# Preparing the feed-forward weights in eighths, inside the turns of the first attention layer

## The chip, the cores and the metric

The kernel runs on one core of a Trainium2 chip. The metric is the device time of one execution in microseconds (us), as the median of several runs. The engines are TensorE (PE; its weight loads are listed as PEld), VectorE (DVE), ScalarE (ACT), GpSimd (POOL) and SyncE (SP), which only issues transfers. A transfer is issued from the queue of an engine (SPq, ACTq, POOLq) and carried by the core's 16 DMA engines. TensorE's granted clock is given as a share of full speed: 1.00 is 2.4 GHz and 0.50 is 1.2 GHz.

## The reference

Two layers over x of 8 batches x 512 positions x 256 features, float32. What matters here is the first:

```
xn = layernorm(x)
x  = x + attention0(xn) + ffn0(xn)          # then a second layer: x + attention1 + mixture of experts

attention0: c = xn @ W_DKV (64 wide); k, v from c; q = xn @ W_UQ
            16 heads of 16, causal, softmax, @ W_O
ffn0:       tlin(x, w, s) = einsum('bsi,oi->bso', x, w) * s
            h = silu(tlin(x, w1)) * tlin(x, w2)         # 256 -> 1024, twice
            h = gelu(tlin(h, h1)); h = gelu(tlin(h, h2)) # 1024 -> 1024
            return tlin(h, w3)                          # 1024 -> 256
```

The weights w1, w2, h1, h2 and w3 hold only -1, 0 and 1 in the inputs used, but the kernel doesn't assume it: it tests at run time whether rounding them loses anything.

## The kernel before

Matrix products keep float32 accuracy by splitting each operand into a rounded part (type fp32r, "high") and what is left ("low"), and adding the products of the parts.

**Layer 0's attention (`latent_attention`)** is a software pipeline over batches. A turn is one batch: 32 steps (`STEPS`), and in each step one score tile (`score`: PE L521 and L526 into PSUM, then the row maximum on DVE, L429) and one probability tile of 13 steps earlier (`prob`: PE L545, exponential on ACT L372, causal cut on POOL L323, and later the value product PE L557). Everything else of a batch is hung on fixed steps by hand, in the table `placed`: loading and normalising the next x (steps 0 to 11), its transpose (`x_turn`, `x_copy`, `x_high`, `x_low`, step 12), v (15), the latent (16), the output's transpose (`mix_turn` and what follows, 17), q and k (`qk`, 18 and 21, with DVE casts L422 `qk_high` and POOL subtractions L313 `qk_low`, 19 and 22), the output product (`out`, 24: PE L483 with l_wo) and its store (`store`, 25, issued by ACT L389). Each engine walks the same list in the same order, and waits only on semaphores, so an instruction put into a step delays all that stands behind it on its engine. Three PSUM slots of two banks go round among `score`, `prob`, `x_turn`, `v`, `qk`, `heads_turn`, `mix_turn` and `out`: a product may start when the reader of the slot three uses back is done (`claim`). So score 21 waits for DVE's maximum of score 20, `out` for that of score 22, and a score whose slot held a probability tile waits for ACT's exponential. The turns are written out for -1, 0, 7 and 8 and looped for 1 to 6.

**Between attention and feed-forward** `clear` resets the semaphores of the attention. Then `ffn` runs three blocks, with all engines meeting between them. The first loads the five weight matrices in 28 chunks of up to 128x1024 into a ring of four (SP L1157), rounds each (ACT L1173), and compares it with its rounding in both directions (DVE L1186, `tensor_tensor_reduce`, which subtracts and keeps the maximum). A transpose on PE (L1207) and two reductions give `flag`, whether anything was lost. The weights' high parts stay in SBUF. Meanwhile `BiasTable` makes a position table for layer 1: POOL loads `wpos`, `coeffs` and `fir` (`t_fir`, 101 rows of 4 KB, L1088), PE multiplies (L1095, L1098), ACT copies (L1103, L1106). The second block writes the low parts to DRAM, if `flag` says so; here it does not. The third loops over the 8 batches: gates and ups (PE L1376, 64 products), h1 and h2 (L1401 with the high part of h, L1411 with the low), w3 (L1446).

Of the kernel before, what the change touches and what calls it, by code (L numbers as in the profile page):

```python
# [15 lines left out]
F32 = mybir.dt.float32  # L16
# [6 lines left out]
P = 128  # L23
B, T, D = 8, 512, 256
KD = D // P
# [70 lines left out]
def latent_attention(nc, x_d, out_d, xh_d, xl_d, w, c):  # L96
# [4 lines left out]
    with ExitStack() as ctx:  # L101
# [40 lines left out]

        slots = [ctx.enter_context(nc.psum_tensor(f"l0_slot{j}", [P, 2, T], F32)) for j in range(3)]
# [24 lines left out]
        out_saved = sem("out_saved", 1, grant=1, unit=16)  # L168
        held_sp, held_dve, held_pool = sem("held_sp"), sem("held_dve"), sem("held_pool")
# [91 lines left out]
        with nc.Block() as block:  # L261
            @block.sync
            def _(sp):
# [34 lines left out]
                sp.dma_start(stacks[HROWS - 1:P:HROWS, 1].bitcast(F32), minus).then_inc(keyed.sem, 16)  # L298
                turns(sp, emit)
# [31 lines left out]
            def _(act):  # L331
# [18 lines left out]
                def emit(kind, b, n, i):  # L350
# [36 lines left out]
                    if kind == "store":  # L387
                        wait(act, out_ready, 1, b)
                        act.dma_start(out_d[b].rearrange("(t p) d -> p t d", p=P), out_sb[:]).then_inc(out_saved.sem, 16)  # L389
                turns(act, emit)  # L390
                act.wait_ge(out_saved.sem, out_saved.at(1, B - 1))

            @block.vector
            def _(dve):
                def emit(kind, b, n, i):
                    if kind == "ln_stats":
# [67 lines left out]
                dve.tensor_tensor(wo[:, 1], raw_wo[:], wo[:, 0].bitcast(F32), ALU.subtract).then_inc(w_ready.sem, 1)  # L464
                turns(dve, emit)

# [122 lines left out]
        clear(nc, tallies)  # L589
# [468 lines left out]

def attention(nc, tag, layer, x_d, out_d, xh_d, xl_d, xn_d, w, c):
    if layer == 0:  # L1060
        latent_attention(nc, x_d, out_d, xh_d, xl_d, w, c)
# [5 lines left out]
class BiasTable:  # L1067
# [5 lines left out]
    def __init__(self, nc, ctx, wpos, coeffs, ext_d, c, banks):  # L1073
        def sb(name, shape):
            return ctx.enter_context(nc.sbuf_tensor(f"t_{name}", shape, F32))

        def sem(name):
            return ctx.enter_context(nc.semaphore(f"t_{name}"))
# [4 lines left out]
        self.loaded, self.cw_ps, self.cw_ready, self.ext_ps, self.ext_ready, self.saved = \  # L1083
            (sem(n) for n in ("loaded", "cw_ps", "cw_ready", "ext_ps", "ext_ready", "saved"))

    def move(self, eng):
        for dst, src in zip((self.wpos, self.coeffs, self.fir), self.sources):
            eng.dma_start(dst[:], src).then_inc(self.loaded, 16)  # L1088
        eng.wait_ge(self.ext_ready, 2)
        eng.dma_start(self.ext_d, self.ext[:].rearrange("h a t -> h (a t)")).then_inc(self.saved, 16)  # L1090
        eng.wait_ge(self.saved, 16)
# [17 lines left out]
def ffn(nc, x_d, attn_d, xh_d, xl_d, out_d, w, c, lo_d, bias):  # L1109
# [5 lines left out]
    with ExitStack() as ctx:  # L1115
        def sb(name, shape, dt=F32):
            return ctx.enter_context(nc.sbuf_tensor(f"f_{name}", shape, dt))

# [6 lines left out]
        names = ("w1", "w2", "h1", "h2", "w3")  # L1125
        wide = {"w1": HID, "w2": HID, "h1": HID, "h2": HID, "w3": D}
        deep = {"w1": KD, "w2": KD, "h1": KH, "h2": KH, "w3": KH}
        hi = {m: sb(f"hi_{m}", [P, deep[m], wide[m]], F32R) for m in names}
        gate_s, both_s, h1_s, h2_s = (sb(n, [P, KH]) for n in ("gate_s", "both_s", "h1_s", "h2_s"))
        out_s = sb("out_s", [P, D])  # L1130
        ident = sb("ident", [P, P])
        flag = sb("flag", [1, 1], mybir.dt.int32)
        low = sb("low", [P, 2, KH, P], F32R)
        psum = [ctx.enter_context(nc.psum_tensor(f"f_ps{j}", [P, T], F32)) for j in range(8)]


        CH, RING = 1024, 4
        chunks = [(m, k) for m in names for k in range(deep[m])]

        loaded = [sem(f"loaded{j}", unit=16) for j in range(RING)]  # L1140
        hi_done, compared = sem("hi_done"), sem("compared")
        raw_in = [sem(f"raw_in{j}", unit=16) for j in range(2)]
        saved = [sem(f"saved{j}", unit=16) for j in range(2)]
        lo_done = sem("lo_done")
        s_in, s_done, peak_ps, peak_done = sem("s_in", unit=16), sem("s_done"), sem("peak_ps"), sem("peak_done")
        with nc.sbuf_tensor("f_raw", [P, RING, CH], F32) as raw, nc.sbuf_tensor("f_junk", [P, 2, CH], F32) as junk, \
             nc.sbuf_tensor("f_peaks", [P, 2, len(chunks)], F32) as peaks, \
             nc.sbuf_tensor("f_peak", [P, 1], F32) as peak, nc.sbuf_tensor("f_any", [1, 1], F32) as top, \
             ExitStack() as inner, nc.Block() as block:
            table = BiasTable(nc, inner, *bias, c, psum[1:4])  # L1150

            @block.sync
            def _(sp):
# [6 lines left out]
            @block.gpsimd  # L1160
            def _(pool):
                pool.dma_start(ident[:], c["c_ident"]).then_inc(s_in.sem, 16)
                for dst, src in ((gate_s, "w1_s"), (both_s, "w2_s"), (h1_s, "h1_s"), (h2_s, "h2_s")):
                    pool.dma_start(dst[:], w[src]).then_inc(s_in.sem, 16)
                s3 = w["w3_s"]
                pool.dma_start(out_s[:], bass.AP(s3.tensor, s3.offset, [[0, P], [1, D]])).then_inc(s_in.sem, 16)
                table.move(pool)

            @block.scalar
            def _(act):  # L1170
                for n, (m, k) in enumerate(chunks):
                    act.wait_ge(loaded[n % RING].sem, 16 * (n // RING + 1))
                    act.activation(hi[m][:, k], raw[:, n % RING, 0:wide[m]], ACT.Copy).then_inc(hi_done.sem, 1)  # L1173
                    if n == len(chunks) // 2:
                        table.copies(act)

            @block.vector
            def _(dve):
                for n, (m, k) in enumerate(chunks):
                    dve.wait_ge(hi_done.sem, n + 1)  # L1180
                    if n:
                        dve.wait_ge(compared.sem, n)

                    pair = raw[:, n % RING, 0:wide[m]], hi[m][:, k].bitcast(F32)
# [822 lines left out]
```

## Time and profile before

| | |
|---|---|
| median of 3 runs | 2241.44 us (2241.33 to 2242.36) |
| the profiled execution | 2235.95 us |
| its span, first to last instruction | 2234.3 us |
| mean granted clock of TensorE | 0.895 |
| busy shares of the span | PE 79%, DVE 50%, ACT 46%, POOL 45% |

The span is from the first instruction to the last; the execution's own time is 1.65 us more, and the median of the plain runs lies 5.5 us above the profiled execution. Times in the rows further down count from the span's start, so attention 0 fills roughly 0 to 504 us, the preparation of the weights 511 to 576, and the feed-forward loop begins at 584.

### The profile page before, as it was taken

The page shows a single profiled execution, that of the slowest core. Times are in us where ns is not written, and L with a number is a line of the kernel's source. Part 1 is how long each engine was busy: PE and PEld are TensorE (multiplying, and loading weights), DVE is VectorE, ACT ScalarE, POOL GpSimd, SP SyncE. Part 2 cuts the span into 40 slices and gives each one's busy share as a digit, 9 for nine tenths or more (in the row PEclk, how much of TensorE's full clock was granted, in tenths as well). Part 3 has the DMA queues.
Part 4 walks back from the last instruction along what each step waited for, and adds up shares of the span by engine and source line. Part 5 has one row for each costly group of instructions (what it writes and reads, how often), then busy time and mean ns, then how long its engine had stood idle before and what let it go on. Part 6 is the DMA issues. An engine that isn't in the chain of part 4 may idle for free. (4 is left out here: it accounts for less than half of the span.)

```text
span 2234.3 us, 33907 instructions
## 1 busy us (share of the span) xinstructions
PE 1764.3 (79%) x10759; PEld 1101.2 (49%) x10759; DVE 1122.0 (50%) x2399; ACT 1024.8 (46%) x1356; POOL 1012.5 (45%) x778
## 2 busy tenths in 40 slices
PE   3888889870599999999999638887887888747933
PEld 2455555540387787787787523333433433235510
DVE  3666666537513313313313148878787787437211
ACT  1455555543313322222223117877787788813400
POOL 3344444320234344343333407777777677724212
PEclk8899999985799999999999858989998999869965
DMA  3333333306201101101100253222222222043999
GB/s 102 87 96 94 94 104 91 94 11 202 84 1 47 47 0 47 47 0 47 45 2 28 77 174 86 67 71 80 80 66 71 81 65 59 10 173 137 345 318 330
DMA packets 129732, 204.38 MB, mean 91 GB/s; under 512 B 14303, under 2 KB 84063, under 8 KB 129668
## 3 DMA queue, kind: packets, MB, share of 16 engines
q1 hardware_dynamic: 107896, 163.40, 24.6%
q10 hardware_dynamic: 16096, 20.65, 2.6%
q0 software_dynamic: 5680, 19.57, 2.2%
q8 instruction: 32, 0.52, 0.1%
q14 instruction: 28, 0.23, 0.0%
HBM read 95.96 MB, written 56.69 MB: 68 GB/s over the span
## 5 line engine op out<-in xcount | busy, mean ns | idle before, releaser
L761 POOL TENSOR_TENSOR l_prob<-l_prob,l_bias 128x1024 f32<-128x1024 f32 x192 | 452.1, 2375 | 149.2 <-ACT l_prob L865 148.4
L1315 POOL TENSOR_TENSOR f_hl<-f_full,f_hh 128x512 fp32r<-128x512 f32 x192 | 247.6, 1290 | 439.9 <-DVE f_hh L1357 283.2
L922 DVE CUSTOM_DVE_ANT_0 l_slot<-l_slot,l_bias 128x512 f32<-128x512 f32 x512 | 340.4, 714 | 52.8 <-PE l_slot L999 51.7
L1357 DVE CAST f_hh<-f_full 128x512 fp32r<-128x512 f32 x128 | 74.8, 585 | 397.7 <-ACT f_full L1336 396.2
L868 ACT ACTIVATE l_prob<-l_prob 128x1024 f32<-128x1024 f32 x256 | 271.1, 1071 | 0.0
L1401 PE MATMUL f_ps<-f_hh,f_hi_h 128*128 128x512 f32 x1024 | 267.1, 397 | 0.0
L1411 PE MATMUL f_ps<-f_hl,f_hi_h 128*128 128x512 f32 x1024 | 265.8, 396 | 0.0
L429 DVE TENSOR_REDUCE l_peak<-l_slot 128x2 f32<-128x256 f32 (+3 forms) x256 | 206.2, 821 | 111.3 <-PE l_slot L526 109.0
L1336 ACT ACTIVATE f_full<-f_ps,f_h_s 128x512 f32<-128x512 f32 x128 | 86.3, 687 | 332.6 <-PE f_ps L1411 308.9
L372 ACT ACTIVATE l_prob<-l_slot 128x1024 f32<-128x1024 f32 (+3 forms) x256 | 174.7, 706 | 96.3 <-PE l_slot L545 93.4
L1401 PEld LDWEIGHTS f_ps<-f_hh,f_hi_h 128*128 128x128 f32 x1024 | 192.8, 188 | 49.3 <-ACT f_hh L1329 2.7
L1411 PEld LDWEIGHTS f_ps<-f_hl,f_hi_h 128*128 128x128 f32 x1024 | 192.9, 188 | 46.6
L865 ACT COPY l_prob<-l_slot 128x1024 f32<-128x1024 f32 x192 | 194.8, 1015 | 34.3 <-PE l_slot L1015 33.6
L323 POOL TENSOR_SCALAR_AFFINE_SELECT l_prob<-l_prob 128x256 f32<-128x256 f32 x256 | 105.0, 418 | 210.1 <-ACT l_prob L372 207.3
L1027 PE MATMUL l_o_bank<-l_prob,l_vals 128*32 128x512 f32 x1024 | 158.3, 694 | 4.7 <-ACT l_prob L868 4.7
L999 PE MATMUL l_slot<-l_stacks 63*128 63x512 f32 x512 | 121.1, 472 | 49.2 <-DVE l_prob L761 23.6
L1015 PE MATMUL l_slot<-l_stacks 64*128 64x512 f32 x512 | 134.5, 524 | 20.9 <-DVE l_peak L922 16.8
L521 PE MATMUL l_slot<-l_stacks 63*128 63x256 f32 (+2 forms) x512 | 98.1, 380 | 32.5 <-ACT l_prob L372 18.1
L1015 PEld LDWEIGHTS l_slot<-l_stacks 64*128 64x128 f32 x512 | 51.5, 199 | 138.3 <-DVE l_peak L922 96.3
L545 PE MATMUL l_slot<-l_stacks 64*128 64x256 f32 (+2 forms) x512 | 109.7, 428 | 10.5 <-DVE l_peak L429 4.1
L557 PE MATMUL l_o_bank<-l_prob,l_vals 128*32 128x512 f32 (+3 forms) x1024 | 97.2, 452 | 11.1 <-POOL l_prob L323 9.7
L1325 ACT ACTIVATE f_tanh<-f_ps,f_gate_s 128x512 f32<-128x512 f32 x64 | 44.1, 688 | 119.5 <-PE f_ps L1376 119.5
(209 smaller groups left out, 2691.5 us busy)
## 6 DMA issues: line engine op xcount, KB each, us to landing
l_stacks<-l_parts SPq DMA_DIRECT2D x384, 128.0 KB, 2.7
inter<-e_stage POOLq DMA_DIRECT2D x32, 512.0 KB, 5.1
c_rows<-inter SPq DMA_DIRECT2D x32, 512.0 KB, 9.6
attn<-l_out_sb ACTq DMA_DIRECT2D x16, 512.0 KB, 2.8
f_raw<-in_L_ffn_h_w SPq DMA_DIRECT2D x16, 512.0 KB, 4.2
e_w<-in_L_ffn_f SPq DMA_DIRECT2D x32, 256.0 KB, 4.4
l_bias<-ext ACTq DMA_DIRECT2D x16, 448.0 KB, 11.8
l_x_in<-in_L_attn_x SPq DMA_DIRECT2D x8, 512.0 KB, 3.8
```

The source lines that it names most:

```text
L372: act.activation(prob[:, n // 2 % RING, 2 * pr:2 * pr + 2, j * P:T], slot(kind, n)[:, :, j * P - q0:wide], ACT.Exp).then_inc(p_exp.sem, 1)
L429: dve.tensor_reduce(peak[:, g, :, pr, t], slot(kind, n)[:, :, 0:(t + 1) * P], AX_X, ALU.max)\
L761: return eng.tensor_tensor(probs(n), src, bias[:, h:h + 2, j * P:j * P + T], ALU.add)
L865: act.copy(probs(n), slot(kind, n)[:]).then_inc(p_copied.sem, 1)
L868: act.activation(probs(n), probs(n), ACT.Exp).then_inc(p_exp.sem, 1)
L922: ins = dve.tensor_tensor_reduce(src, src, bias[:, 4 * g + 2 * pr + a, t * P:t * P + T], 1.0, 3 * NEG, ALU.add, ALU.max, peak[:, g, a, pr, ...
L999: ins = pe.matmul(out[:, a], stacks[r, 0, 2 * g + pr, t * P:(t + 1) * P], stacks[r, 1, 2 * g + pr, ::-1], start=True, stop=True)
L1015: ins = pe.matmul(out[:, a], stacks[r, 1, 2 * g + pr, j * P:(j + 1) * P], stacks[r, 0, 2 * g + pr, ::-1], start=True, stop=True)
L1027: ins = pe.matmul(o_bank[32 * a:32 * a + 32, :], vals_sb[:, v0:v0 + 32], prob[:, n % RING, a], start=(j == 0), stop=(j == TT - 1), skip_gr ...
L1315: pool.tensor_tensor(hl[layer % 2][:, o], full[:, n % 2], hh[layer % 2][:, o].bitcast(F32), ALU.subtract).then_inc(h_lo.sem, 1)
L1401: ins = pe.matmul(hidden[n % 4][:], hi[m][:, k, cut], hh[layer % 2][:, k], start=(k == 0), stop=False, skip_group_check=True)
L1411: ins = pe.matmul(hidden[n % 4][:], hi[m][:, k, cut], hl[layer % 2][:, k], start=False, stop=(k == KH - 1), skip_group_check=True)
```

## The change

The preparation block and the block for the low parts go. Each turn of layer 0's attention now prepares an eighth of every weight matrix (`Prepare`; a row block of 128 of w3, h1 and h2, and a column block of 128 of w1 and w2: 2816 columns in all): ACT issues five loads in step 7, rounds four cuts of 704 columns in steps 12, 13, 15 and 16, and stores the high part in step 18 and the low part in step 26; DVE makes the low part and one maximum in steps 14, 16, 19 and 21, and the maximum of the opposite difference in steps 15, 18, 20 and 22. Both parts are always written, to DRAM. After the last turn the flag is made.

The feed-forward stage is now one block. SP loads x and then the high parts of all weights from DRAM, and PE waits for each where it first needs it. The position table moves into this block: its three loads from POOL's queue to ACT's, its products on PE ahead of the first gate product. The semaphores of the attention are cleared by POOL within the same block, so one meeting of the engines is left between the two stages.

```diff
+        for s, kind, n in ((7, "f_load", 0), (12, "f_round", 0), (13, "f_round", 1), (15, "f_round", 2), (16, "f_round", 3),
+                           (14, "f_low", 0), (15, "f_high", 0), (16, "f_low", 1), (18, "f_high", 1),
+                           (19, "f_low", 2), (20, "f_high", 2), (21, "f_low", 3), (22, "f_high", 3),
+                           (18, "f_save_high", 0), (26, "f_save_low", 0), (27, "f_worst", 0)):
+            placed[s].append((kind, 0, n))
         for s, events in {0: [("x_load", 1, 0)],
...
+                    if kind == "f_load":
+                        wait(act, f_compared, 2 * prep.SPLIT, b - 1)
+                        for m in prep.NAMES:
+                            dst = f_raw[:, prep.columns(m)]
+                            if m in ("w1", "w2"):
+                                dst = dst.rearrange("p (k n) -> p k n", k=KD)
+                            act.dma_start(dst, prep.source(m, b)).then_inc(f_loaded.sem, 16)
+                    if kind == "f_round":
+                        if n == 0:
+                            wait(act, f_loaded, len(prep.NAMES), b)
+                            wait(act, f_saved, 2, b - 1)
+                        cut = slice(n * cut_by, (n + 1) * cut_by)
+                        act.copy(f_high[:, cut], f_raw[:, cut]).then_inc(f_rounded.sem, 1)
+                    if kind == "f_save_high":
+                        wait(act, f_rounded, prep.SPLIT, b)
+                        act.dma_start(prep.high_d[b], f_high[:].bitcast(F32)).then_inc(f_saved.sem, 16)
+                    if kind == "f_save_low":
+                        wait(act, f_compared, 2 * prep.SPLIT, b)
+                        act.dma_start(prep.low_d[b], f_low[:]).then_inc(f_saved.sem, 16)
...
+                            hold(dve, held_dve, f_rounded, n + 1, b)
+                            dve.tensor_tensor_reduce(f_low[:, cut], pair[0], pair[1], 1.0, 0.0, ALU.subtract, ALU.max,
+                                                     peaks[:, 0, n:n + 1]).then_inc(f_compared.sem, 1)
+                        else:
+                            hold(dve, held_dve, f_compared, 2 * n, b)
+                            dve.tensor_tensor_reduce(junk[:], pair[1], pair[0], 1.0, 0.0, ALU.subtract, ALU.max,
+                                                     peaks[:, 1, n:n + 1]).then_inc(f_compared.sem, 1)
...
-        clear(nc, tallies)
+    return tallies
...
-            table = BiasTable(nc, inner, *bias, c, psum[1:4])
-                for n, (m, k) in enumerate(chunks):
-                    if n >= RING:
-                        sp.wait_ge(compared.sem, n - RING + 1)
-                    sp.dma_start(raw[:, n % RING, 0:wide[m]], w[m + "_w"][k * P:(k + 1) * P])\
-                      .then_inc(loaded[n % RING].sem, 16)
...
-                table.move(pool)
...
-                    act.activation(hi[m][:, k], raw[:, n % RING, 0:wide[m]], ACT.Copy).then_inc(hi_done.sem, 1)
...
+        before = latent_attention(nc, *FIRST.pop(), prep)
...
+                sp.dma_start(gates_flat[:, 0], prep.high_d[0, :, both]).then_inc(first_in.sem, 16)
+                sp.dma_start(gates_flat[:, 1:KH], prep.high_d[1:KH, :, both].rearrange("k p n -> p k n")).then_inc(gates_in.sem, 16)
+                for m in ("h1", "h2", "w3"):
+                    pieces(hi[m][:].bitcast(F32), prep.columns(m), later_in[m].sem)
...
+                for tally in before:
+                    pool.sem_clear(tally.sem)
...
             def _(act):
+                table.load(act)
+                table.copies(act)
+                table.store(act)
                 with act.Fori(0, B) as i:
...
+                table.products(pe)
                 with pe.Fori(0, B) as i:
                     pe.wait_ge(xt_in.sem, xt_in.at(2, i))
                     for o in range(KH):
+                        if o < 2:
+                            pe.wait_ge((first_in, gates_in)[o].sem, 16)
...
+                        pe.wait_ge(later_in[("h1", "h2")[layer]].sem, 16)
```

## Rows read from the trace of the kernel before

**Rows 1.** Busy time by stretch: length, each engine, PEclk, DMA share, GB/s

```profile
222.40:276.74 54.34, 48.01 (x476) 28.05 (x477) 34.80 (x62) 29.80 (x43) 23.35 (x37) 1.00 0.37 97
...
511.40:576.10 64.70, 4.48 (x7) 0.92 (x7) 54.67 (x117) 25.39 (x31) 5.49 (x10) 0.50 0.59 189
```

**Rows 2.** Timeline from the attention's end to the first gate: start, us, work

```profile
503.97 0.39 ACTq L389 DMA_DIRECT2D attn<-l_out_sb  x1
...
511.42 1.78 SPq L1157 DMA_DIRECT2D f_raw<-in_L_ffn_w_w  x4
...
575.88 0.17 DVE L1199 TENSOR_TENSOR f_both_s<-f_gate_s,f_both_s 128x8 f32<-128x8 f32 x1
...
578.98 0.34 SPq L1272 DMA_DIRECT2D f_xh<-xh  x1
...
584.01 2.08 PE L1376 MATMUL f_ps<-f_xl,f_hi_w 128*128 128x512 f32 x4 [8.73 <-DMA f_xl<-xl]
```

**Rows 3.** The position table's work on PE in the preparation block

```profile
521.99 0.51 PE L1095 MATMUL f_ps<-t_wpos,t_coeffs 4*101 4x16 f32 x2 [19.15 <-DMA t_fir<-c_fir]
...
549.47 3.59 PE L1098 MATMUL f_ps<-t_fir,t_cw 101*16 101x512 f32 x4 [26.97 <-ACT t_cw L1103]
```

**Rows 4.** Transfers: KB, us to landing; packets in 12.4 to 12.8; in 1283.5 to 1290

```profile
attn<-l_out_sb ACTq DMA_DIRECT2D x16, 512.0 KB, 2.8
...
t_fir<-c_fir POOLq DMA_DIRECT2D x1, 404.0 KB, 5.6
...
q1 hardware_dynamic: 2, 0.03, 38.3%
...
DMA packets 1235, 2.62 MB, mean 403 GB/s; under 512 B 105, under 2 KB 675, under 8 KB 1232
```

**Rows 5.** ACT and PE around step 7 of one turn

```profile
269.14 0.58 ACT L377 COPY l_o_sb<-l_o_bank 128x512 f32<-128x512 f32 x1
269.62 0.82 ACT L372 ACTIVATE l_prob<-l_slot 128x768 f32<-128x768 f32 x1
270.49 0.19 PEld L521 LDWEIGHTS l_slot<-l_stacks 63*128 63x128 f32 x2 [0.20 <-ACT l_prob L372]
```

**Rows 6.** Rounding and comparing: ns min/median/max

```profile
L1173 ACT ACTIVATE f_hi_h<-f_raw x16: 1040/1057/1057, 523.0 to 561.3; 128x1024 fp32r<-128x1024 f32 x16
...
L1186 DVE CUSTOM_DVE_ANT_0 f_junk<-f_raw,f_hi_h x16: 1224/1225/1226, 526.4 to 564.8; 128x1024 f32<-128x1024 f32 x16
L1186 DVE CUSTOM_DVE_ANT_0 f_junk<-f_raw,f_hi_w x12: 424/426/1226, 516.3 to 573.7; 128x256 f32<-128x256 f32 x8, 128x1024 f32<-128x1024 f32 x4
```

**Rows 7.** A DVE operation with two SBUF inputs beside POOL's, in layer 1's selection

```profile
1992.88 0.69 DVE L1626 TENSOR_TENSOR s_perm<-s_logits,s_best 128x512 f32<-128x512 f32 x1
...
2004.10 2.37 POOL L1572 TENSOR_TENSOR s_tl<-s_xn,s_th 128x1024 fp32r<-128x1024 f32 x1 [8.21 <-ACT s_th L1597]
...
2006.05 0.99 DVE L1626 TENSOR_TENSOR s_perm<-s_logits,s_best 128x512 f32<-128x512 f32 x1
```

**Rows 8.** DVE, POOL and PE in steps 14 to 24 of one turn

```profile
278.64 2.35 POOL L310 TENSOR_TENSOR l_xl<-l_x_full,l_xh 128x1024 fp32r<-128x1024 f32 x1 [2.65 <-DVE l_xh L413]
...
291.13 2.38 POOL L317 TENSOR_TENSOR l_mixt<-l_mix_full,l_mixt 128x1024 fp32r<-128x1024 f32 x1 [2.57 <-DVE l_mixt L425]
...
291.16 1.20 DVE L429 TENSOR_REDUCE l_peak<-l_slot 128x2 f32<-128x1024 f32 x1
293.08 0.69 DVE L429 TENSOR_REDUCE l_peak<-l_slot 128x2 f32<-128x512 f32 x1 [0.72 <-PE l_slot L526]
293.69 0.72 DVE L422 CAST l_parts<-l_qk_full 128x1024 fp32r<-128x1024 f32 x1
294.69 1.29 DVE L429 TENSOR_REDUCE l_peak<-l_slot 128x2 f32<-128x768 f32 x2 [0.28 <-PE l_slot L526]
...
298.10 0.39 PE L521 MATMUL l_slot<-l_stacks 63*128 63x512 f32 x2
...
301.29 3.10 PE L483 MATMUL l_slot<-l_wo,l_mixt 128*128 128x256 f32 x24
```

More of the change, by code:

```diff
@@ L93, in _, with __init__, columns, source @@
                 sp.sem_clear(tally.sem)
-def latent_attention(nc, x_d, out_d, xh_d, xl_d, w, c):
+class Prepare:
+    NAMES, SPLIT = ("w1", "w2", "w3", "h1", "h2"), 4
+    def __init__(self, w, high_d, low_d, scales, out_s, flag):
+        self.w, self.high_d, self.low_d, self.scales, self.out_s, self.flag = w, high_d, low_d, scales, out_s, flag
+        self.wide = {"w1": KD * P, "w2": KD * P, "w3": D, "h1": HID, "h2": HID}
+        self.at, self.total = {}, 0
+        for m in self.NAMES:
+            self.at[m] = self.total
+            self.total += self.wide[m]
+    def columns(self, m):
+        return slice(self.at[m], self.at[m] + self.wide[m])
+    def source(self, m, b):
+        ap = self.w[m + "_w"]
+        if m in ("w1", "w2"):
+            return ap.rearrange("(k p) n -> p k n", p=P)[:, :, bass.ds(b * P, P)]
+        return ap[bass.ds(b * P, P)]
+def latent_attention(nc, x_d, out_d, xh_d, xl_d, w, c, prep):
     with ExitStack() as ctx:
@@ L1133, in ffn @@
[L1133 to L1144, printed above, removed]
@@ L1258, in ffn, with sb @@
         half_gated = sem("half_gated", KH)
+        first_in, gates_in = sem("first_in", unit=16), sem("gates_in", unit=16)
+        later_in = {m: sem(f"{m}_in", unit=16) for m in ("h1", "h2", "w3")}
+        table_sems = [sem(f"t_{n}").sem for n in BiasTable.SEMS]
+        scales = {m: ctx.enter_context(nc.sbuf_tensor(f"f_{m}_s", [P, KH], F32)) for m in ("w1", "w2", "h1", "h2")}
+        out_s = ctx.enter_context(nc.sbuf_tensor("f_out_s", [P, D], F32))
+        flag = ctx.enter_context(nc.sbuf_tensor("f_flag", [1, 1], mybir.dt.int32))
+        prep = Prepare(w, *(nc.dram_tensor(f"weights_{n}", [B, P, 2 * KD * P + D + 2 * HID], F32, kind=SCRATCH).ap()
+                            for n in ("high", "low")), scales, out_s, flag)
+        gate_s, both_s, h1_s, h2_s = (scales[m] for m in ("w1", "w2", "h1", "h2"))
+        before = latent_attention(nc, *FIRST.pop(), prep)
+        def sb(name, shape, dt=F32):
+            return room.enter_context(nc.sbuf_tensor(f"f_{name}", shape, dt))
+        gate_w = sb("gate_w", [P, KH, 2, KD, P], F32R)
+        hi = {m: sb(f"hi_{m}", [P, KH, n], F32R) for m, n in (("h1", HID), ("h2", HID), ("w3", D))}
+        low = sb("low", [P, 2, KH, P], F32R)
+        psum = [room.enter_context(nc.psum_tensor(f"f_ps{j}", [P, T], F32)) for j in range(8)]
+        table = BiasTable(nc, room, *bias, c, psum[5:8], table_sems)
+        xh, xl = sb("xh", [P, KD, T], F32R), sb("xl", [P, KD, T], F32R)
+        x_in, attn = sb("x_in", [P, TT, D]), sb("attn", [P, TT, D])
+        out_sb = sb("out_sb", [P, TT, D])
+        tanh = sb("tanh", [P, 2, T])
+        gated = sb("gated", [P, 2, T])
+        full = sb("full", [P, 2, T])
+        hh = [sb(f"hh{j}", [P, KH, T], F32R) for j in range(2)]
+        hl = [sb(f"hl{j}", [P, KH, T], F32R) for j in range(2)]
         gates, ups, hidden, outs = psum[0:2], psum[2:4], psum[4:6] + psum[2:4], psum[6:8]
@@ L1386, in _ @@
                         two = [gates[o % 2][:], ups[o % 2][:]]
-                        products(two, [[(hi[m][:, k, cut], xl[:, k]) for k in range(KD)] for m in ("w1", "w2")], True, False)
+                        products(two, [[(gate_w[:, o, m, k], xl[:, k]) for k in range(KD)] for m in range(2)], True, False)
                         with pe.If(any_low == 1):
@@ L1392, in _ @@
                                      False, False).then_inc(lo_used.sem, 2)
-                        products(two, [[(hi[m][:, k, cut], xh[:, k]) for k in range(KD)] for m in ("w1", "w2")],
+                        products(two, [[(gate_w[:, o, m, k], xh[:, k]) for k in range(KD)] for m in range(2)],
                                  False, True).then_inc(gu_ps.sem, 1)
```

173 lines of the change are left out of this document (66 added, 107 removed).

## The prediction

> **What bounds the kernel now.** I read the busy time by stretch first. In a steady turn of layer 0's attention, 54.34 us, PE is busy 48.01, DVE 34.80, ACT 29.80 and POOL 23.35 [rows 1]: PE sets the pace, and the others have room by their sums. The preparation block is the opposite: in 64.70 us PE works 4.48 and DVE 54.67. Then I read the timeline at the seam. ACT issues the last store at 503.97; the first weight chunk is asked for at 511.42; the last scaling ends at 576.05; x is asked for at 578.98; the first gate product starts at 584.01 [rows 2]. From 504 to 584 nothing is done that the change keeps in place, so this is the gain's ceiling: 80 us. Last I read the order of time of DVE, POOL and ACT inside one turn, since the change puts its work there, and the position table and the DMA rows, since the change moves the table ahead of the first gate.
>
> **The seam, removed.** The last store is issued by 504.4 and lands 2.8 us after its issue began [rows 4], at 506.8. One meeting of engines is left, with a read of the flag. The nearest price is 576.05 to 578.98, 2.93 us for two block ends and their flag reads [rows 2]; half is 1.5. So SP asks for x at 508.3 instead of 578.98. By itself that would be worth 70.7 us. The flag's transpose and reductions lie beside the last store's landing: nothing. Clearing the attention's semaphores lies on POOL, which has no work until the first h: nothing.
>
> **The seam, added: the position table.** PE now makes it before the first gate, and its third load, t_fir, comes from ACT's queue, asked for some 0.8 us after the block starts (two issues before it at 0.39 [rows 2]), at 509.1. After its landing PE needs 0.51 us, a copy on ACT that I take at 0.4 with its hand-overs, and 3.59 us for L1098 [rows 3]: 4.5 us. What is the landing? From POOL's queue the same 404 KB landed in 5.6 us [rows 4]: the lower bound. Then PE starts the gates at 509.1 + 5.6 + 4.5 = 519.2, and the seam gives 584.01 - 519.2 = 64.8 us. For the upper bound: on SP's hardware queue a two-row transfer of 32 KB (the rows of -1 put into the stacks at the start) left two packets, one a row [rows 4], so this queue deals out rows and does not cut them; ACT's is of the same kind. 101 rows can't be dealt evenly over 16 engines. If they go through one engine, the price follows from the saturated stretch: 403 GB/s over 16 engines is 25 GB/s each [rows 4], and 414 KB at 25 GB/s is 16.5 us. SP's loads are queued on all engines at once (x, 1 MB, then 11.5 MB of weights, over 30 us at 403 GB/s), so that engine serves two queues in turn: 33 us. With 1.5 us of latency (a 512 KB store landed in 2.8, of which 1.3 is data at 403 GB/s [rows 4]) the table lands at 509.1 + 34.5 = 543.6 and the gates start at 548.1: the seam gives 35.9 us. I take this end: the two-row transfer is the nearest row in kind of queue, the 5.6 us row only in bytes.
>
> What the row alone can't decide, a page does. The Trainium skill (DMA: Bandwidth & Descriptors, "Why a DMA increments its semaphore by 16 and not by 1") says that the hardware queues use the largest number of engines up to 16 that divides the count of the slowest dimension, and that GpSimd's queue is excepted for some direct copies. 101 is prime, so by that rule it is one engine and the seam gives the smaller sum; by the 5.6 us row it would be the larger one. No row here shows a 101-row transfer on ACT's queue.
>
> The weights themselves are no wait: x, w1, w2 and h1 are 7.3 MB, 18 us at 403 GB/s, and with half speed on the shared engine some 36 us, by 546; the gates only begin at 548.1. h2 and w3 follow in 13 us, and are needed later.
>
> **The turns, added.** Per turn ACT gets seven issues (0.39 to 0.45 us each: L1157 has four in 1.78 [rows 2]) and four roundings of 704 columns (1.06 us for 1024 [rows 6], so 0.75): 5.9 us. DVE gets eight compares of 704 (0.42 us at 256 columns, 1.22 at 1024 [rows 6]: 0.89 each): 7.1 us. If all lay on the path: 13.0 a turn, 104 in eight. If none did: nothing. The sums of rows 1 would allow nothing, but the order doesn't.
>
> *Step 7.* The five issues stand behind the copy of the heads, which starts at 269.14, and ahead of the exponential that ran at 269.62. Five take 2.2 us, so that exponential starts at 271.4, 1.8 late. PE was waiting on just this exponential (0.20 us at 270.49 [rows 5]), so PE pays 1.8. The loads (1.44 MB, 3.6 us and latency) land by about 277; with the 1.8 us shift rounding 0 is needed at 277.7: no more.
>
> *Two SBUF inputs.* A DVE operation with two SBUF inputs took 0.69 us alone, and 0.99 us when it began at 2006.05 under a POOL operation that ran from 2004.10 to 2006.47 [rows 7]: it waits until POOL is done. The compares have two such inputs, and each also keeps POOL out for its 0.89.
>
> *Step 14.* L310 holds POOL to 280.99 [rows 8]; the first compare goes next and POOL's cuts behind it, for which PE's value product waits: 0.8. Roundings 1 and 2 on ACT push its copies by about 0.3 where it has no gap.
>
> *Steps 18 to 24* [rows 8]. DVE's maximum 17 ends at 292.3. The compare waits for L317 until 293.5, ends 294.4; maximum 18 (0.69) 295.0; compare 295.9; cast L422 296.6, which frees POOL's L313, 2.4 us, to 299.0; maximum 19 297.5; the compare of step 20 waits to 299.0 and ends 299.9; maximum 20, 300.3. PE's score 21 ran at 298.10: 2.2 late. Then POOL's two cuts, compare, maximum 21 to 302.8, compare, cast, maximum 22 to 305.1. The output product waits for it, and ran at 301.29: 3.8 late in all. Without the lock the same chain ends at 302.1: 0.8 late.
>
> A full turn pays 1.8 + 0.8 + 0.3 + 3.8 = 6.7; six are 40. Turn 0 has no exponential in step 7 and no L317: about 3. Turn 7 has no next x: 1.8 + 2.5. The turns cost 47 us. Stores and loads (4.3 MB a turn) beside a DMA share of 0.37 I count at nothing; the stack transfers have over ten steps of room.
>
> **Sum.** -35.9 + 47 = +11. The profiled execution would go from 2235.95 to 2247 (span 2234.3 to 2245.4). The median of the runs lies 5.5 us above that execution; from 2241.44 the sum gives 2252.5.
>
> **Rivals.**
> *The table lands fast* (20%). If ACT's queue spreads 101 rows as POOL's did, the seam gives 64.8: 2241.4 - 64.8 + 47 = 2224, faster. It decides alone: with turns at 47, the kernel is faster by over 0.2% once t_fir lands within 19 us of its issue. For it: the 5.6 us row. Against: that is another kind of queue.
> *The turns are cheap* (17%). DVE idles 19.5 of 54.3 us in a turn; if the compares find it, only step 7 and 0.8 us of the DVE chain are paid, 18 us in all, up to 30: 2224 to 2236. Against: the lock of rows 7.
> *The two cancel* (12%). One engine, turns at 30 to 40: within 0.2%, which is 4.5 us and about what a measurement of this kernel can tell from no change.
> *The turns are dear* (13%). Over 62 us, up to 104 if every added instruction is paid: 2268 to 2310. The small transfers of the row maxima behind the 1.4 MB stores of steps 18 and 26 would add to it.
> *My forecast* (38%): one engine, turns at 40 to 62, 2246 to 2268.
>
> **How the numbers follow.** Faster: 17% and, of the fast table's 20%, 16%: 0.33. Same: 12% and 2%: 0.14. Slower: 38 + 13 + 2%: 0.53. The range 2218 to 2273 leaves out the dearer turns (about 10%) and the best of the fast tables (about 7%). For my own case alone it is 2246 to 2268.
>
> **What the changed profile would show.** First, the landing of t_fir in the transfer list: near 35 us or near 6; and PE's wait ahead of L1095 in the new block. x asked for about 1.5 us after the last store lands. A steady turn of 61 us instead of 54.3; PE waiting for ACT's exponential of step 7 by some 2 us; compares that last 1 to 2.4 us instead of 0.89 where POOL runs L313, L317 or L310; and the output product late behind maximum 22. The prediction is wrong if t_fir lands fast, if the compares are all 0.89 us and a turn stays under 57 us, or if the first h1 product waits for its weights.

## The result, and the profile after

The changed kernel takes 2294.78 us (median of 4 runs, 2293.06 to 2299.17), the kernel before 2241.39 us (4 runs, 2237.09 to 2242.36): ratio 1.0242, interval 1.0223 to 1.026. It is slower by 53.4 us. I had forecast +11 and a range up to 2273; the sign was right and the size was far off, outside the range. The profiled execution took 2293.52 us, its span is 2291.9.

First the seam, in the timeline of the changed kernel (start, us, work):

```profile
608.46 0.39 ACTq L431 DMA_DIRECT2D attn<-l_out_sb  x1
...
612.71 0.35 SPq L1279 DMA_DIRECT2D f_xh<-xh  x1
612.74 0.27 ACTq L1187 DMA_DIRECT2D t_fir<-c_fir  x1
...
644.17 0.51 PE L1198 MATMUL f_ps<-t_wpos,t_coeffs 4*101 4x16 f32 x2 [36.74 <-DMA t_fir<-c_fir]
...
648.48 2.08 PE L1398 MATMUL f_ps<-f_xl,f_gate_w 128*128 128x512 f32 x4
```

From the last store's issue to x asked for are 4.25 us (I had 4.3), from t_fir's issue to PE's first product with the table 31.4 (34.5 forecast for its landing), from there to the gates 4.3 (4.5). The whole seam is 40.0 us instead of the 80.0 of [rows 2]: it gives 40.0, where I had 35.9.

The loss is in the turns. Windows of the changed kernel: one steady turn, and under it slices of the same turn; the row of the kernel before is in [rows 1]. Columns: stretch and length, busy PE, PEld, DVE, ACT, POOL, granted clock, DMA share, GB/s.

```profile
297.62:366.00 68.38, 56.30 (x476) 32.65 (x478) 44.78 (x79) 32.77 (x47) 25.71 (x37) 0.85 0.47 140
```
```profile
297.62:302.50 4.88, 4.67 (x53) 2.14 (x53) 2.77 (x6) 3.30 (x5) 1.22 (x3) 1.00 0.59 218
302.50:307.39 4.89, 2.81 (x26) 1.45 (x26) 1.89 (x3) 1.59 (x3) 0.86 (x3) 0.86 0.95 283
307.39:312.27 4.88, 4.88 (x36) 3.28 (x38) 2.73 (x6) 2.24 (x4) 1.17 (x3) 0.50 0.60 172
312.27:317.16 4.89, 4.59 (x49) 2.02 (x47) 3.48 (x8) 2.30 (x5) 1.22 (x3) 0.94 0.01 2
317.16:322.04 4.88, 3.88 (x48) 2.11 (x48) 4.68 (x13) 2.88 (x4) 2.03 (x4) 1.00 0.57 130
322.04:326.93 4.89, 2.46 (x16) 0.66 (x14) 1.64 (x4) 1.51 (x2) 1.38 (x4) 0.61 0.91 258
326.93:331.81 4.88, 4.88 (x35) 2.28 (x33) 2.88 (x5) 1.34 (x3) 0.81 (x2) 0.50 0.18 70
```

This turn is 68.38 us, the one of [rows 1] 54.34. PE runs the same 476 matmuls in both. Its idle time rose from 6.3 to 12.1 us, and its busy time from 48.0 to 56.3, because the granted clock of the turn fell from 1.00 to 0.85 (56.30 times 0.85 is 47.9). The slices show how: full clock, then a slice in which PE stalls and works 2.81 us, then a slice at 0.50 (the 1.2 GHz level) in which PE is busy all the time and gets through 36 matmuls (53 in the first slice, in other shapes). The same comes again at 322. So 8.3 of the 14.0 us between these two turns are not waits at all, and the sum in the prediction had no term for them.

The kernel before is not at full clock in all its turns, though, so single turns overstate the difference. Here are another of its turns, and then both kernels, before and changed, from the start to the last output copy:

```profile
304.48:360.98 56.50, 50.66 (x476) 30.17 (x478) 34.80 (x62) 29.80 (x44) 23.34 (x37) 0.94 0.35 93
```
```profile
0.00:502.93 502.93, 407.35 (x3792) 240.93 (x3792) 282.53 (x504) 241.95 (x352) 197.66 (x302) 0.94 0.32 86
```
```profile
0.00:607.41 607.41, 458.78 (x3793) 267.55 (x3793) 360.31 (x644) 265.37 (x383) 214.90 (x302) 0.84 0.42 128
```

Over the whole attention the change adds 104.5 us, 53.1 as idle time of PE and 51.4 as busy time. Over the five turns from the first output copy to the sixth the mean goes from 55.24 to 68.28 us: 13.0 a turn, half of it busy time. The turn at 0.94 has the same waits as the turns at 1.00, none over 1.3 us, so the clock also falls at times without an added stall.

These are the two stalls in the timeline. The first, at step 29, is PE waiting for the row maxima. SP asked for them in two transfers of 4 KB, one at 299.67 and one at about 300.4; ACT's store of the low parts was issued between the two:

```profile
299.67 1.42 SPq L326 DMA_DIRECT2D l_stacks<-l_tops  x2
...
299.92 0.34 ACTq L450 DMA_DIRECT2D weights_low<-l_f_low  x1
...
305.55 0.50 PE L640 MATMUL l_slot<-l_stacks 64*128 64x512 f32 x2 [2.01 <-DMA l_stacks<-l_tops]
```

The second is step 7 of the next turn, the one that I had costed at 1.8 us. Compare the same two products in the kernel before, where L521 (now L616) waited 0.20 us [rows 5]:

```profile
321.06 1.54 ACTq L438 DMA_DIRECT2D l_f_raw<-in_L_ffn_w_w  x3
322.76 0.87 ACTq L438 DMA_DIRECT2D l_f_raw<-in_L_ffn_h_w  x2
323.82 1.51 ACT L414 ACTIVATE l_prob<-l_slot 128x768 f32<-128x768 f32 x2 [2.39 <-issue]
```
```profile
324.68 0.58 PE L616 MATMUL l_slot<-l_stacks 63*128 63x256 f32 x2 [2.43 <-ACT l_prob L414]
325.06 0.38 PE L621 MATMUL l_slot<-l_half_b 64*128 64x128 bf16 x4
325.38 1.93 PE L652 MATMUL l_o_bank<-l_prob,l_vals 128*32 128x512 f32 x8
```

The eight value matmuls of this shape that took 1.93 us here took 1.06 at 298.05 of the same kernel, at full clock. And the compares beside POOL, in steps 18 to 22 of the same kernel:

```profile
282.65 1.98 DVE L470 CUSTOM_DVE_ANT_0 l_junk<-l_f_high,l_f_raw 128x704 f32<-128x704 f32 x1
...
286.74 2.37 POOL L355 TENSOR_TENSOR l_parts<-l_qk_full,l_parts 128x1024 fp32r<-128x1024 f32 x1 [1.48 <-DVE l_parts L502]
287.44 2.41 DVE L470 CUSTOM_DVE_ANT_0 l_junk<-l_f_high,l_f_raw 128x704 f32<-128x704 f32 x1
...
292.29 0.88 DVE L470 CUSTOM_DVE_ANT_0 l_junk<-l_f_high,l_f_raw 128x704 f32<-128x704 f32 x1
...
294.43 3.10 PE L578 MATMUL l_slot<-l_wo,l_mixt 128*128 128x256 f32 x24 [1.20 <-DVE l_peak L509]
```

Alone a compare takes 0.88 us (0.89 forecast). Begun under a POOL operation, it ends some 0.7 us after POOL's, and takes up to 2.41.

The account of the profiled executions: the copy of the last output product starts at 607.41 instead of 502.93, so the turns cost 104.5 us (20.6 up to the first output copy, 77.8 over the next six, 6.1 in the last); the seam gives 40.0; from the first gate to the end it is 1643.4 instead of 1650.3, 6.9 less. 104.5 - 40.0 - 6.9 = 57.6, the difference of the spans. The kernels below that share the stage behind the gates took 1643.4 to 1651.8 there (2228.5 less 585.09 with the three moves, 2275.1 less 623.26 with the table on POOL's queue), so I read nothing into the 6.9.

### The profile page after: what moved, and what is told of

It is laid out like the page before. It is cut to its first block and busy times, and to the rows that moved or that the text cites. A ratio compares the mean times of both kernels' runs of the same rounds, so it can differ in the third digit from the quotient of the medians.

```text
span 2291.9 us, 34111 instructions
## 1 busy us (share of the span) xinstructions
PE 1806.2 (79%) x10759; PEld 1123.4 (49%) x10759; DVE 1144.4 (50%) x2424; ACT 1023.3 (45%) x1360; POOL 1024.4 (45%) x768
## 5 line engine op out<-in xcount | busy, mean ns | idle before, releaser
L1333 POOL TENSOR_TENSOR f_hl<-f_full,f_hh 128x512 fp32r<-128x512 f32 x192 | 247.7, 1290 | 452.9 <-DVE f_hh L1379 281.4
L1020 DVE CUSTOM_DVE_ANT_0 l_slot<-l_slot,l_bias 128x512 f32<-128x512 f32 x512 | 340.4, 714 | 51.4 <-PE l_slot L1097 50.5
L365 POOL TENSOR_SCALAR_AFFINE_SELECT l_prob<-l_prob 128x256 f32<-128x256 f32 x256 | 122.1, 484 | 268.5 <-ACT l_prob L414 266.9
L616 PE MATMUL l_slot<-l_stacks 63*128 63x256 f32 (+2 forms) x512 | 108.8, 421 | 49.3 <-ACT l_prob L414 30.6
L640 PE MATMUL l_slot<-l_stacks 64*128 64x256 f32 (+2 forms) x512 | 120.6, 468 | 28.1 <-DMA l_stacks<-l_tops 18.0
L652 PE MATMUL l_o_bank<-l_prob,l_vals 128*32 128x512 f32 (+3 forms) x1024 | 109.6, 504 | 14.0 <-POOL l_prob L365 13.0
L1113 PEld LDWEIGHTS l_slot<-l_stacks 64*128 64x128 f32 x512 | 50.8, 196 | 137.3 <-DVE l_peak L1020 94.2
L640 PEld LDWEIGHTS l_slot<-l_stacks 64*128 64x128 f32 x512 | 54.2, 208 | 93.6 <-issue 50.6
```

Source lines behind the costliest of these rows:

```text
L640: ins = pe.matmul(out[:, a, 0:wide], stacks[r, 1, 2 * g + pr, j * P:(j + 1) * P], stacks[r, 0, 2 * g + pr, q0:T], start=True, stop=True)
L1020: ins = dve.tensor_tensor_reduce(src, src, bias[:, 4 * g + 2 * pr + a, t * P:t * P + T], 1.0, 3 * NEG, ALU.add, ALU.max, peak[:, g, a, pr, ...
L1113: ins = pe.matmul(out[:, a], stacks[r, 1, 2 * g + pr, j * P:(j + 1) * P], stacks[r, 0, 2 * g + pr, ::-1], start=True, stop=True)
L1333: pool.tensor_tensor(hl[layer % 2][:, o], full[:, n % 2], hh[layer % 2][:, o].bitcast(F32), ALU.subtract).then_inc(h_lo.sem, 1)
```

## The experiments

Theory: every cost of the turns is a stall of PE followed by matmuls at the lower clock; the stalls come from step 7's issues, from the maxima behind the low store, and from DVE and POOL keeping each other out; and the table is late because its transfer from ACT's queue is slow. The first four runs undo one part each. Medians are of 4 runs unless said otherwise. Since single turns differ in clock, this table has each profiled execution up to its last output copy (us; the last column is the mean of the five turns between the first output copy and the sixth):

| kernel | last output copy | PE busy | PE idle | a turn |
|---|---|---|---|---|
| before | 502.9 | 407.4 | 95.6 | 55.24 |
| changed | 607.4 | 458.8 | 148.6 | 68.28 |
| changed, loads by SP | 580.4 | 444.5 | 136.0 | 64.85 |
| changed, no compares | 572.2 | 444.6 | 127.5 | 64.16 |
| changed, low store moved | 580.2 | 443.2 | 137.0 | 64.83 |
| before, with the loads alone | 529.3 | 414.5 | 114.8 | 58.68 |
| before, with one ACT copy | 526.1 | 422.4 | 103.7 | 58.65 |
| three moves | 567.8 | 431.9 | 135.9 | 63.60 |
| three moves, compares spread | 546.8 | 430.3 | 116.5 | 60.36 |
| the same, loads in step 5 | 519.1 | 418.6 | 100.5 | 56.64 |

**The table's queue.** The three loads are issued by POOL instead of ACT:

```diff
             def _(pool):
+                table.load(pool)
...
             def _(act):
-                table.load(act)
```

> The changed kernel, with the position table's three loads issued by POOL instead of ACT, nothing else moved. One-engine theory: from ACT's queue the 101 rows of 404 KB landed 31.3 us after their issue and the gates waited for the table's products; from POOL's queue they land in about 6, and the gates then start when their first 256 KB of weights is in (11.7 us after its issue in the changed kernel), some 20 to 23 us earlier: 2294.8 to about 2273. A steady turn stays at 68.4 us. Rival, the weights in flight set the landing (t_fir is late because 13 MB share the engines with it, whatever the queue): it lands after 25 us or more and the time stays over 2288.

Measured: 2274.83 us, 1.0148 of before (1.0121 to 1.0175), 20.0 less than the changed kernel. Landing in us, at the end of each row, first the changed kernel, then this one:

```profile
f_hi_h<-weights_high SPq DMA_DIRECT2D x2, 4096.0 KB, 42.0
...
f_gate_w<-weights_high SPq DMA_DIRECT2D x1, 1792.0 KB, 27.3
```
```profile
f_hi_h<-weights_high SPq DMA_DIRECT2D x2, 4096.0 KB, 26.6
...
f_gate_w<-weights_high SPq DMA_DIRECT2D x1, 1792.0 KB, 11.2
...
t_fir<-c_fir POOLq DMA_DIRECT2D x1, 404.0 KB, 7.2
```

The gates start at 623.26, 16.8 us after the last store's issue at 606.48; the seam gives 63.3, close to the 64.8 of "the table lands fast". The turn stays at 68.4. SP's weights landed sooner too, though nothing of theirs was changed: the gates' weights and those of h1 and h2 some 15 us, the last ones (w3) 2 us. With t_fir on ACT's queue, something that they all need was held up. That fits one engine serving both queues, and not 13 MB in flight as such, which are there in this kernel as well. (The Trainium skill, DMA: Bandwidth & Descriptors, "Why a DMA increments its semaphore by 16 and not by 1", gives a rule by which the 101 rows, a prime number, go through one engine; the runs agree with what follows from it, though no row names the engine.)

**The issues of step 7.** SP issues the five loads (the block stands in SP's order of events instead of ACT's):

```diff
                     if kind == "f_load":
...
-                            act.dma_start(dst, prep.source(m, b)).then_inc(f_loaded.sem, 16)
+                            sp.dma_start(dst, prep.source(m, b)).then_inc(f_loaded.sem, 16)
```

> The changed kernel, with the five weight loads of step 7 issued by SP instead of ACT. In the changed kernel PE waits 2.4 us in step 7 for the exponential behind the five issues, and its matmuls of the next steps run at a lower granted clock. Stall-and-clock theory: what a stall costs is its length and about as much again in slow matmuls; seven turns lose 2.4 + 2.4 us or a little more: -34, to about 2261. Rival, stall alone (the clock is low for another reason, the added work of all engines): -13 to -17, to about 2280, granted clock in a steady turn unchanged at 0.85. Rival, SP's queue is no freer: its transfers of the row maxima and of x come later and PE waits for them instead; no gain, over 2288.

Measured: 2272.11 us, 1.0133 (1.0102 to 1.0165), 22.7 less. Its turn, by windows:

```profile
284.43:349.11 64.68, 53.47 (x476) 31.57 (x478) 44.69 (x79) 32.71 (x47) 25.65 (x37) 0.89 0.49 148
```

3.7 us less in this turn, of which 2.8 are busy time of PE: the clock rose from 0.85 to 0.89. The mean turn is 3.4 shorter, 2.2 of it busy time. "Stall alone" (0.85 kept) falls. The gain is 11 short of the 34 expected; PE now waits 7.7 us in all for ACT's copy of the turned x, against 0.4 in the changed kernel.

**No compares.** The eight compares are taken out.

```diff
-                           (14, "f_low", 0), (15, "f_high", 0), (16, "f_low", 1), (18, "f_high", 1),
-                           (19, "f_low", 2), (20, "f_high", 2), (21, "f_low", 3), (22, "f_high", 3),
...
-                        act.dma_start(prep.low_d[b], f_low[:]).then_inc(f_saved.sem, 16)
...
+                        act.dma_start(prep.low_d[b], f_raw[:]).then_inc(f_saved.sem, 16)
```

> The changed kernel without the eight compares a turn on DVE; it leaves out the low parts (the store of step 26 writes the raw weights, as many bytes) and the flag stays at zero. Lock theory: the compares and POOL's operations keep each other from starting; they cause the stalls at steps 14 and 18 to 24, 4.6 us of the 5.7 us of added idle time of PE, and by the clock most of the 8.3 us of added busy time: a turn falls from 68.4 to about 58 and the kernel to about 2215. Rival, the transfers and the issues (ACT's five loads, the row maxima behind the stores) are what costs: a turn stays over 65 and the kernel over 2265.

Measured: 2262.25 us, 1.009 (1.0057 to 1.0122), 32.5 less, just under the rival's 2265 and far from the lock theory's 2215. Two turns, the third and the fifth of the five:

```profile
283.14:348.04 64.90, 55.85 (x476) 32.57 (x478) 34.98 (x62) 32.62 (x47) 23.47 (x37) 0.84 0.49 148
```
```profile
410.92:472.86 61.94, 51.34 (x476) 29.82 (x478) 34.81 (x62) 32.51 (x47) 23.55 (x37) 0.92 0.51 155
```

In the first of them 3.5 us are gone, 3.0 of them idle time, and busy time and clock stay where they were. Over the five turns it is 4.1 a turn, 2.9 of idle and 1.2 of busy time. So the waits that the compares cause are somewhat less than forecast (4.6 in steps 14 and 18 to 24), and most of the lower clock does not come from them, as I had expected it would. The two long stalls are left in this kernel, and behind each of them a slice of the first turn is at 0.50, as before. They stand in the second turn too, as long (2.0 and 2.4 us), and there the clock is 0.92: how much slow time a stall brings differs from turn to turn.

**The low store moved** to step 4 of the next turn.

```diff
-                           (18, "f_save_high", 0), (26, "f_save_low", 0), (27, "f_worst", 0)):
-            placed[s].append((kind, 0, n))
+                           (18, "f_save_high", 0), (4, "f_save_low", 0), (27, "f_worst", 0)):
+            placed[s].append((kind, -1 if kind == "f_save_low" else 0, n))
```

> The changed kernel, with the store of the low parts (1408 KB) moved from step 26 to step 4 of the next turn, where no row maxima are in flight; all work is kept. Transfer theory: over the kernel PE waits 18.0 us for the stacks that take the row maxima, in step 29 behind the store of step 26, and nothing before the change; with the store gone from there the wait goes, and with it slow matmuls of about its size: -25 to -35, to 2260 to 2270. Rival, the store only meets other small transfers at step 4: the same wait under another step, within 5 us of 2294.8. Rival, the wait goes but PE then waits for something else that is as late: under 10 us gained.

Measured: 2270.06 us, 1.0136 (1.0106 to 1.0166), 24.7 less. The page's row of the products that need the maxima, first the changed kernel, then this one (the last figures: idle ahead of them and what ended it), and the turn:

```profile
L640 PE MATMUL l_slot<-l_stacks 64*128 64x256 f32 (+2 forms) x512 | 120.6, 468 | 28.1 <-DMA l_stacks<-l_tops 18.0 <-DVE l_peak L509 6.4 <-ACT l_prob L414 2.4
```
```profile
L640 PE MATMUL l_slot<-l_stacks 64*128 64x256 f32 (+2 forms) x512 | 114.6, 447 | 9.9 <-DVE l_peak L509 5.8 <-ACT l_prob L414 2.4 <-ACT l_x_full L396 0.4
```
```profile
287.66:352.52 64.86, 53.50 (x476) 31.01 (x478) 44.72 (x79) 32.48 (x48) 25.72 (x37) 0.89 0.47 148
```

The turn is 3.5 us shorter, and so is the mean. The wait of 18.0 us is gone (0.3 is left), the clock is up to 0.89, and the transfer theory stands, with 24.7 just under its 25 to 35. The store is not free at step 4, though: the five issues of step 7, on the same queue, now take 3.2 us instead of 2.4, and the stall there grew from 2.4 to 3.1 us.

**One part alone, on the kernel before.** Two kernels ask whether the clock follows the stall. The first has only ACT's five loads in step 7, into a tile that nothing reads; the second, in their place, one ACT copy of 2048 columns between two idle tiles:

```diff
+                    if kind == "f_load":
...
+                        act.copy(f_dst[:], f_src[:]).then_inc(f_idle.sem, 1)
```

> The kernel before, with one part of the change alone: ACT issues the five weight loads (1.44 MB a turn) in step 7 into a tile that nothing reads. Stall-and-clock theory: PE waits about 2 us for the exponential behind the issues, and its matmuls of the next steps run at a lower granted clock, which costs as much again or a little less: a steady turn of about 58 instead of 54.34, seven turns dearer by 3.6: 2241 to about 2266. Rival, stall alone: 56.2 a turn, about 2254. Rival, a single stall a turn is soaked up by the gaps that PE has anyway (6.3 us a turn): under 2248.

> The kernel before, with one ACT copy of 2048 columns (about 2.1 us, from one idle tile to another) in step 7, and nothing moved by DMA. If what costs in the loads' kernel is ACT's time ahead of the exponential and PE's clock after it, this one costs the same as that: within 5 us of it, about 2264, steady turn about 58. If the transfers of the 1.44 MB (contention with the stack transfers and the row maxima) are the cost, this one is cheaper by 8 us or more.

Measured: 2265.64 us, 1.0093 (1.0064 to 1.0122), and 2261.41, 1.0083 (1.0052 to 1.0115). Turns of the one and of the other:

```profile
263.24:321.38 58.14, 49.37 (x476) 28.41 (x478) 34.73 (x62) 29.98 (x44) 23.50 (x37) 0.97 0.42 116
```
```profile
262.69:321.79 59.10, 51.74 (x476) 29.77 (x478) 34.91 (x62) 31.68 (x45) 23.47 (x37) 0.91 0.33 89
```

Both came out as expected (2266, and within 5 us of it). The copy took 1.90 us in the trace and moved nothing by DMA, yet the mean turn is 3.4 us longer with it: 2.4 as busy time of PE at the lower clock and 1.0 as idle time. That is the cleanest showing of the missing term. The loads' kernel, with 2.4 us of ACT's time, pays 3.4 a turn too, but 2.4 of it as idle time and 1.0 as busy time, so the share of the clock is not fixed. By the medians the two kernels are 22.1 and 17.9 us over the kernel before (2243.53 in the same set of runs). Their times overlap (2262.19 to 2268.51 and 2259.15 to 2268.14), so they cost the same within what this tells. The 1.44 MB themselves are not what costs in step 7.

**The three moves together** (POOL's queue for the table, SP for the loads, the low store at step 4), and then the same with the compares where DVE and POOL both had gaps:

```diff
-                           (14, "f_low", 0), (15, "f_high", 0), (16, "f_low", 1), (18, "f_high", 1),
-                           (19, "f_low", 2), (20, "f_high", 2), (21, "f_low", 3), (22, "f_high", 3),
...
+                           (15, "f_low", 0), (15, "f_low", 1), (17, "f_high", 0), (17, "f_low", 2),
+                           (21, "f_low", 3), (24, "f_high", 1), (24, "f_high", 2), (28, "f_high", 3),
```

> The changed kernel with three moves together, all work kept: the table's loads on POOL's queue, the five weight loads issued by SP, the store of the low parts in step 4 of the next turn. Alone they gave 20, 22.7 and 24.7 us below 2294.8. If the stalls are separate and each carries its own slow matmuls, the gains add: 67 less, about 2227, a steady turn of about 61, faster than before the change by 0.6%. Rival, the clock does not come back while the compares still stall PE, or one wait takes another's place: the gains overlap, 35 to 50 in all, 2245 to 2260.

> The three moves together, and the eight compares placed where DVE and POOL both had gaps in the kernel before: steps 15, 15, 17, 17, 21, 24, 24 and 28 instead of 14 to 16 and 18 to 22. Lock theory: the compares no longer meet POOL's 2.4 us operations and no longer push the maxima of steps 18 to 22; leaving them out altogether gave 32.5 us, and this should give two thirds of it: 20 below the three moves alone, about 2207, a turn of 58 or less. Rival, what the compares cost is the 7.1 us of DVE's time near the maxima wherever they stand: within 6 us of the three moves alone.

Measured: 2237.04 us (10 runs), 0.9974 of before (0.9959 to 0.9988), and 2216.89, 0.9861 (0.9825 to 0.9897). The three moves gave 57.7 of the 67.4 that they gave one by one, between the 2227 of added gains and the 2245 to 2260 of the rival; the kernel before read some 2 us higher in this set of runs, so the overlap is known to a few us only. Spreading the compares gave 20.2 more, the 20 expected; the 2207 was missed by the 10 us that the three moves lacked. What was still missing shows in the trace of the spread kernel:

```profile
295.00 1.58 SPq L312 DMA_DIRECT2D l_f_raw<-in_L_ffn_w_w  x3
...
302.86 0.78 ACT L444 CAST l_f_high<-l_f_raw 128x704 fp32r<-128x704 f32 x1 [3.28 <-DMA l_f_raw<-in_L_ffn_h_w]
303.55 1.00 ACT L403 COPY l_x_full<-l_slot 128x1024 f32<-128x1024 f32 x1
...
304.68 0.79 PE L640 MATMUL l_slot<-l_stacks 64*128 64x512 f32 x2 [2.57 <-ACT l_x_full L403]
```

Without the old stalls step 12 comes sooner, and the weights asked for in step 7 are late for the first rounding; the copy of the turned x is queued behind that, and PE behind the copy: a new wait of 24.6 us in all. So the loads go to step 5; the last kernel also puts the roundings into steps 13, 14, 15 and 17:

```diff
-        for s, kind, n in ((7, "f_load", 0), (12, "f_round", 0), (13, "f_round", 1), (15, "f_round", 2), (16, "f_round", 3),
...
+        for s, kind, n in ((5, "f_load", 0), (13, "f_round", 0), (14, "f_round", 1), (15, "f_round", 2), (17, "f_round", 3),
```

> The spread kernel (three moves, compares spread), with SP issuing the five weight loads in step 5 instead of step 7. In the spread kernel the last load lands 5.3 us after its issue began, ACT waits for it in front of the first rounding, its copy of the turned x stands behind that, and PE waited 24.6 us for that copy over the kernel. Theory: two steps earlier (some 4 us) the loads are there, that wait goes with its slow matmuls, 3 to 4.5 us a turn: 2216.9 to about 2190. Rival, SP's other transfers are pushed instead or the copy is late by the rounding's own 0.78 us: under 8 us gained.

> As the kernel with the loads in step 5, and the four roundings on ACT in steps 13, 14, 15 and 17 instead of 12, 13, 15 and 16, so that none stands ahead of the copy of the turned x. If the rounding's 0.78 us in front of that copy still delays PE, another 5 to 8 us go, to about 2184; the rival is that the compares of step 15 then meet the later roundings and nothing is gained, within 4 us of the other kernel.

Measured (5 runs each): 2190.14 us, 0.9783 (0.9757 to 0.9808), and 2186.27, 0.9756 (0.9735 to 0.9777). The first is 26.8 us below the spread kernel, where about 2190 was expected. The second is not told apart from the first, as its rival had it: its runs (2182.47 to 2187.86) overlap the first's (2183.26 to 2198.9), and its steady turns are no shorter. One turn of the kernel with the loads in step 5, and the row of its products that had waited:

```profile
262.35:318.63 56.28, 49.61 (x476) 29.31 (x478) 43.47 (x80) 32.35 (x48) 26.78 (x38) 0.97 0.54 171
```
```profile
L640 PE MATMUL l_slot<-l_stacks 64*128 64x256 f32 (+2 forms) x512 | 112.2, 437 | 12.9 <-DVE l_peak L509 6.4 <-ACT l_prob L421 2.4 <-ACT l_qk_full L410 2.4
```

The turn is 1.9 us over that of [rows 1], the mean turn 1.4 us over the mean of before, with 8.7 us more work on DVE, 2.6 on ACT and the same 4.3 MB of added transfers. Its clock is 0.97. The turns cost 16.2 us in all (last output copy at 519.09 against 502.93), and the seam is 17.8 us from that copy to the gates against 81.1. This version beats both kernels: the idea of the change is worth 2.2%, its placement made it cost 2.4%.

## Why the prediction was wrong

**The turns added** is the step that failed: "A full turn pays 1.8 + 0.8 + 0.3 + 3.8 = 6.7". It summed waits and priced PE's own work at the duration of [rows 1], at clock 1.00. The turns were to cost 47 us, all of it waits. Measured are 104.5: 53.1 us of idle time of PE, near the 47, and 51.4 us of busy time at a lower clock, for which there was no term. The ACT copy of 1.90 us, alone on the kernel before, shows that term by itself: 15.0 of its 23.1 us up to the last output copy are busy time. (The Trainium skill, TensorE: Matmul & The Clock Gate, "HAM oscillation — how this bites in real kernels", tells of a kernel that pays for the lower clock again at each recurring wait. The waits there are longer, some 3 to 5 us. The trace agrees that the price recurs, and has it behind shorter waits: 0.50 in the slice behind each of two stalls of 2.0 and 2.4 us. I did not weigh it.)

That the waits came near their 47 us is partly luck, since errors cancel. Here are PE's two rows of score and probability products over the whole kernel, before and then changed (L640 of the changed kernel stands above):

```profile
L545 PE MATMUL l_slot<-l_stacks 64*128 64x256 f32 (+2 forms) x512 | 109.7, 428 | 10.5 <-DVE l_peak L429 4.1 <-ACT l_prob L372 2.4 <-ACT l_qk_full L361 2.4
L521 PE MATMUL l_slot<-l_stacks 63*128 63x256 f32 (+2 forms) x512 | 98.1, 380 | 32.5 <-ACT l_prob L372 18.1 <-DMA l_stacks<-l_parts 8.7 <-DVE l_peak L429 4.6
```
```profile
L616 PE MATMUL l_slot<-l_stacks 63*128 63x256 f32 (+2 forms) x512 | 108.8, 421 | 49.3 <-ACT l_prob L414 30.6 <-DMA l_stacks<-l_parts 13.4 <-DVE l_peak L509 3.4
```

*Step 7* was right: 1.8 forecast, 2.2 measured (2.43 against 0.20), and over the kernel 12.5 us more waiting for ACT's exponentials. Moving the issues away gave 3.4 a turn with the clock's share. *Two SBUF inputs*, steps 14 and 18 to 24: 4.6 forecast. Without the compares a turn has 2.9 us less idle time, so the mechanism was right and the size too high.

**"Stores and loads ... I count at nothing"** was wrong for one of them. The low store of step 26 held up the row maxima: 18.0 us of waiting over the kernel (0.3 before), 24.7 us in time when it was moved. I had named this beside the rival "the turns are dear" and given it no price. Nor had the sum a term for the start: up to the first output copy, which is turn 0 and most of turn 1, the kernel is 20.6 us late, where it had about 3 for turn 0 and 6.7 for turn 1. Of that, 4.7 us are PE's wait for its first stack transfer (13.4 instead of 8.7).

The rival "the turns are dear" (2268 to 2310, 13%) is what came. That its upper end, 104 if every added instruction is paid, meets the measured 104.5 is chance: nearly the same instructions, five issues of them on SP, cost 16.2 us in the kernel with the loads in step 5.

**The seam** was right: x asked for within 0.1 us of the forecast, t_fir 0.8 us sooner, its landing by ACT's queue 31.4 instead of 34.5, the seam 40.0 instead of 35.9. The choice of the slow end over the 5.6 us row was confirmed by the table's own experiment (7.2 us from POOL's queue). "The weights themselves are no wait" held, but they too were slowed: 27.3 us instead of 11.2.

**Left open.** The gains of the moves overlap: the attention is 27.0 and 27.3 us shorter with one of the two and 39.6 with both. The new wait for the turned x (24.2 us with the three moves, 7.7 with the loads on SP alone) fits that in size, and the loads in step 5 removed it. Each of the two long stalls taken away gave back 14.3 and 15.6 us of PE's busy time, both together 26.9. Where the rest of the 51.4 comes from, and why the same stall brings a clock of 0.84 in one turn and 0.92 in another, no run shows. No run holds the clock fixed: that it falls because of the stalls rests on the slices, and on the clock following each change made to the stalls.

## What to carry to other kernels

Where PE sets the pace at full clock, price an added wait by its length plus the slow matmuls behind it, by the windows of a stretch at the lower clock, and take the mean of several turns: here one wait of some 2 us a turn cost 3.4 to 3.5 us in each of four comparisons (loads moved, low store moved, loads added, ACT copy added). Put DMA issues on the queue whose engine nobody waits for, large stores away from small transfers that PE needs soon, and operations with two SBUF inputs where POOL is idle; the same work cost 104 us in one placement and 16 in another. After each stall that is removed read the waits again, since what had been in time by the stall may now be late.

## What the hardware showed that I had not expected

- A single stall of PE of 2.0 us was followed by a slice of 4.9 us at 0.50 of the clock. In the kernel before, the clock of the five turns was 0.94 to 1.00; with one ACT copy of 1.90 us added to each it was 0.91 to 0.94.
- One load of 404 KB in 101 rows on ACT's queue more than doubled the landing time of a 1792 KB load on SP's queue (11.2 to 27.3 us).
- Of two 4 KB transfers the first was asked for 0.25 us ahead of a 1408 KB store on another queue and the second about 0.5 us behind the start of the store's issue. PE, which needed both, went on 5.9 us after the first issue began.
